# Feed forward: the merge of the heads as three float32r products, with rests taken by VectorE

## The reference, cut to what matters

```python
merged = scaled.transpose(0, 2, 1, 3).reshape(B, S, 2 * E)     # 8192 tokens x 512
return merged @ Wo                                             # 512 x 256
...
x = x + _layernorm(_L0_attn_ref(_layernorm(x), ...))
x = x + _layernorm(_L0_ffn_ref(_layernorm(x), W1, b1, W2, b2)) # 256 -> 1024, gelu, -> 256
```

## Time and profile before

| | us |
|---|---|
| median of 3 runs | 3853.26 (3853.02 to 3857.16) |
| the profiled execution's own time | 3850.38 |
| its span in the profile | 3848.7 |
| PE busy in the span | 3415.3 (89%) |
| DVE busy | 2936.1 (76%) |
| ACT busy | 2231.0 (58%) |

### The profile page before, as it was taken

How to read it: one execution, slowest core, us unless ns; L and a number is a source line. 1 busy time by engine, 2 the same in 40 slices (tenths; PEclk the granted TensorE clock), 3 DMA queues, 4 the chain that set the end, 5 groups by cost and what they waited for, 6 DMA issues and landing times. The chain is left out here.

```text
span 3848.7 us, 67900 instructions
## 1 busy us (share of the span) xinstructions
PE 3415.3 (89%) x22102; PEld 2005.8 (52%) x22102; DVE 2936.1 (76%) x7111; ACT 2231.0 (58%) x4709; POOL 1688.8 (44%) x2993
## 2 busy tenths in 40 slices
PE   5886999999999999999999959999698887969950
PEld 4775444444444444444444428888344444648840
DVE  6765999999999999999999916666377776863348
ACT  4554477777777777777777737776101104635532
POOL 2411266666666666666666641111000003656642
PEclk9998899999999999999999989999899997989975
DMA  5777544444443444534434222220410113335668
GB/s 179 227 226 221 82 84 71 77 80 71 78 77 71 80 74 73 80 72 75 82 71 75 41 72 77 88 88 28 140 44 22 44 33 118 117 129 168 176 188 255
DMA packets 377610, 390.26 MB, mean 101 GB/s; under 512 B 118896, under 2 KB 291824, under 8 KB 375216
## 3 DMA queue, kind: packets, MB, share of 16 engines
q1 hardware_dynamic: 362960, 347.42, 39.0%
q0 software_dynamic: 13728, 37.77, 2.6%
q10 hardware_dynamic: 576, 0.79, 0.1%
HBM read 229.17 MB, written 155.05 MB: 100 GB/s over the span
## 5 line engine op out<-in xcount | busy, mean ns | idle before, releaser
L725 ACT ACTIVATE att_p<-att_st 128x512 f32<-128x512 f32 (+3 forms) x3072 | 1325.3, 492 | 472.1 <-PE att_st L662 452.9
L792 DVE TENSOR_REDUCE att_mcol<-att_ring 128x1 f32<-128x512 f32 (+3 forms) x3072 | 1483.1, 547 | 136.3 <-PE att_ring L640 108.6
L662 PE MATMUL att_st<-att_ops 99*128 99x512 bf16 (+3 forms) x3072 | 915.7, 328 | 4.3 <-ACT att_p L725 3.5
L637 PE MATMUL att_ring<-att_ops 96*128 96x512 bf16 (+3 forms) x3072 | 879.2, 332 | 26.1 <-DMA att_va<-values 23.2
L674 PE MATMUL att_pv<-att_p,att_va 128*32 128x512 f32 (+3 forms) x6144 | 603.3, 495 | 2.0 <-POOL att_p L781 1.3
L781 POOL TENSOR_SCALAR_AFFINE_SELECT att_p<-att_p 128x512 f32<-128x512 f32 x512 | 321.8, 634 | 591.9 <-ACT att_p L725 587.0
L662 PEld LDWEIGHTS att_st<-att_ops 99*128 99x128 bf16 x3072 | 284.9, 98 | 446.0 <-ACT att_p L725 278.8
L640 PE MATMUL att_ring<-c_mask,c_identb 128*128 128x128 bf16 x2048 | 435.2, 222 | 0.0
L637 PEld LDWEIGHTS att_ring<-att_ops 96*128 96x128 bf16 x3072 | 296.8, 98 | 205.1 <-DVE att_mcol L792 79.6
L674 PEld LDWEIGHTS att_pv<-att_p,att_va 128*32 128x32 f32 x6144 | 144.7, 109 | 273.0 <-ACT att_p L725 140.8
L640 PEld LDWEIGHTS att_ring<-c_mask,c_identb 128*128 128x128 bf16 x2048 | 202.9, 99 | 106.2 <-issue 0.6
(11 more groups left out here) (269 smaller groups left out, 6073.8 us busy)
## 6 DMA issues: line engine op xcount, KB each, us to landing
att_ops<-parts SPq DMA_DIRECT2D x1524, 64.0 KB, 3.4
parts<-prj_pt SPq DMA_DIRECT2D x128, 384.0 KB, 4.1
moe_work<-moe_rows SPq DMA_DIRECT2D x79, 260.0 KB, 2.9
values<-prj_vs SPq DMA_DIRECT2D x16, 1024.0 KB, 6.6
att_va<-values SPq DMA_DIRECT2D x64, 256.0 KB, 4.2
heads<-att_ofin SPq DMA_DIRECT2D x128, 128.0 KB, 2.3
ffn_os<-heads SPq DMA_DIRECT2D x16, 1024.0 KB, 4.8
moe_work<-x SPq DMA_DIRECT2D x32, 512.0 KB, 4.3
```

Source lines behind the costliest of these rows:

```text
L637: ins = nc.tensor.matmul(ring[k % NB][:, 0:w], ops[0:KR, s, a, mp, i * P:(i + 1) * P], ops[0:KR, s, a, 2 + mp, c * GN:c * GN + w], start=T ...
L662: nc.tensor.matmul(stp[(t * NST + n) % NS][:, off:GN], ops[:, s, a, 2 + mp, j * P:(j + 1) * P], ops[:, s, a, mp, half * GN + off:(half + 1 ...
L725: act.activation(pr[:, g % R, b, off:GN], stp[(t * NST + n) % NS][:, off:GN], ACT.Exp, scale=SCALE).then_inc(exp_done, 1)
L792: v.tensor_reduce(mcol[:, t % 2, c, col:col + 1], ring[k % NB][:, 0:min(GN, (i + 1) * P - c * GN)], AX.X, ALU.max).then_inc(ring_read, 1)
```

## The change

`wo` is split once into a float32r rounded part `woh` (ACT) and the rest `wol` (DVE). ACT's copy of the turned heads now writes `mt` as float32r, and DVE takes the rest `ml = tp - mt` from the PSUM bank (`merged_low`). The merge is three products, `mt` x `woh`, `ml` x `woh` and `mt` x `wol`, 12 float32r matmuls for a token tile instead of 4 float32 ones. The merge waits for all four rests, and the next user of a bank waits for its rest too. ACT waits for the merges of the group before, before it writes `mt[:, 0]`. On DVE eight `merged_low` stand ahead of `merged_stats(0)`, and in each group with one ahead two stand after `low_part` 0 and two after `low_part` 2.

```diff
--- before.py
+++ after.py
@@ -901,7 +901,8 @@
         m = Mem(nc, ctx, "ffn")
         os_ = m.sb("os", [P, 2, GT, H * VD])
         xs = m.sb("xs", [P, 2, GT, E])
-        mt = m.sb("mt", [P, HC, GN])
+        mt, ml = m.sb("mt", [P, HC, GN]), m.sb("ml", [P, HC, GN])
+        woh, wol = m.sb("woh", [P, HC, E]), m.sb("wol", [P, HC, E])
         x1, xn = m.sb("x1", [P, 3, GT, E]), m.sb("xn", [P, 2, GT, E])
         xt, xl = m.sb("xt", [P, 2, EC, GN]), m.sb("xl", [P, 2, EC, GN])
         hf, ht, hl = m.sb("hf", [P, FM, GN]), m.sb("ht", [P, FM, GN]), m.sb("hl", [P, FM, GN])
@@ -910,9 +911,9 @@
         var, rstd, nmr = m.sb("var", [P, 3, GT]), m.sb("rstd", [P, 3, GT]), m.sb("nmr", [P, 3, GT])
         tp, hp, ya, yo = ([m.ps(f"{n}{i}") for i in range(2)] for n in ("tp", "hp", "ya", "yo"))
         h_loaded, x_loaded, x_stored = m.sems("h_loaded", 2), m.sems("x_loaded", 2), m.sems("x_stored", 2)
-        (own_steps, tp_ready, tp_copied, ya_ready, ya_scale, ya_read, x1_ready, x1_scale, xn_ready,
+        (wo_round, wo_rest, ml_ready, own_steps, tp_ready, tp_copied, ya_ready, ya_scale, ya_read, x1_ready, x1_scale, xn_ready,
          xl_ready, hid_ready, gelu_done, lo_ready, yo_ready, yo_read, y_scale, yf_ready, out_ready) = (m.sem(n) for n in (
-            "own_steps", "tp_ready", "tp_copied", "ya_ready", "ya_scale", "ya_read", "x1_ready", "x1_scale",
+            "wo_round", "wo_rest", "ml_ready", "own_steps", "tp_ready", "tp_copied", "ya_ready", "ya_scale", "ya_read", "x1_ready", "x1_scale",
             "xn_ready", "xl_ready", "hid_ready", "gelu_done", "lo_ready", "yo_ready", "yo_read", "y_scale", "yf_ready", "out_ready"))
         power = Power(C, 0)
         chunks, before, last = turn_order()
@@ -968,7 +969,7 @@
 
         @block.tensor
         def _(pe):
-            pe.wait_ge(C["s_ffn"], 48)
+            pe.wait_ge(wo_rest, 1)
 
             def bank_free(g, c):
                 was = last[g, c]
@@ -977,6 +978,8 @@
                 pe.wait_ge(tp_copied, was + 1)
                 if chunks[was][1] >= HC:
                     pe.wait_ge(xl_ready, chunks[was][0] * EC + chunks[was][1] - HC + 1)
+                else:
+                    pe.wait_ge(ml_ready, chunks[was][0] * HC + chunks[was][1] + 1)
 
             def turn_heads(g, c):
                 if c == 0:
@@ -987,12 +990,13 @@
                 ins.then_inc(tp_ready, 1)
 
             def merge(g, t):
-                pe.wait_ge(tp_copied, turned(g, HC - 1))
+                pe.wait_ge(ml_ready, (g + 1) * HC)
                 if g and t % 2 == 0:
                     pe.wait_ge(ya_read, 4 * (g - 1) + 2 * (t // 2) + 2)
-                for c in range(HC):
-                    ins = nc.tensor.matmul(ya[t // 2][:, t % 2 * E:(t % 2 + 1) * E], mt[:, c, t * P:(t + 1) * P],
-                                           C["wo"][:, c], start=(c == 0), stop=(c == HC - 1))
+                for one, (a, w) in enumerate(((mt, woh), (ml, woh), (mt, wol))):
+                    for c in range(HC):
+                        ins = nc.tensor.matmul(ya[t // 2][:, t % 2 * E:(t % 2 + 1) * E], a[:, c, t * P:(t + 1) * P].bitcast(F32R),
+                                               w[:, c].bitcast(F32R), start=(one == 0 and c == 0), stop=(one == 2 and c == HC - 1))
                 ins.then_inc(ya_ready, 1)
 
             def turn_x(g):
@@ -1049,7 +1053,9 @@
         def _(act):
             def merged(g, c):
                 act.wait_ge(tp_ready, turned(g, c))
-                act.activation(mt[:, c], tp[c % 2][:], ACT.Copy).then_inc(tp_copied, 1)
+                if g and c == 0:
+                    act.wait_ge(ya_ready, g * GT)
+                act.activation(mt[:, c].bitcast(F32R), tp[c % 2][:], ACT.Copy).then_inc(tp_copied, 1)
 
             def x_group(g):
                 for c in range(EC):
@@ -1089,6 +1095,8 @@
                 act.activation(hf[:, n], hp[n % 2][:], ACT.Gelu, bias=C["b1"][:, n:n + 1])
                 act.activation(ht[:, n].bitcast(F32R), hp[n % 2][:], ACT.Gelu, bias=C["b1"][:, n:n + 1]).then_inc(gelu_done, 1)
 
+            act.wait_ge(C["s_ffn"], 48)
+            act.activation(woh[:].bitcast(F32R), C["wo"][:], ACT.Copy).then_inc(wo_round, 1)
             for c in range(HC):
                 merged(0, c)
             for c in range(HC):
@@ -1144,6 +1152,10 @@
                     v.wait_ge(tp_copied, turned(g, HC + c))
                     v.tensor_tensor(xl[:, g % 2, c].bitcast(F32R), tp[c % 2][:], xt[:, g % 2, c], ALU.subtract).then_inc(xl_ready, 1)
 
+            def merged_low(g, c):
+                v.wait_ge(tp_copied, turned(g, c))
+                v.tensor_tensor(ml[:, c].bitcast(F32R), tp[c % 2][:], mt[:, c], ALU.subtract).then_inc(ml_ready, 1)
+
             def low_part(g, n):
                 v.wait_ge(gelu_done, g * FM + n + 1)
                 v.tensor_tensor(hl[:, n].bitcast(F32R), hf[:, n], ht[:, n], ALU.subtract).then_inc(lo_ready, 1)
@@ -1168,6 +1180,12 @@
             for k, work in enumerate(power_order()):
                 nth[work, power_order()[:k].count(work)] = k
 
+            v.wait_ge(wo_round, 1)
+            v.tensor_tensor(wol[:].bitcast(F32R), C["wo"][:], woh[:], ALU.subtract).then_inc(wo_rest, 1)
+            for c in range(HC):
+                merged_low(0, c)
+            for c in range(HC):
+                merged_low(1, c)
             merged_stats(0)
             scales(0, nth["a", 0], ya_scale)
             merged_add(0)
@@ -1186,6 +1204,9 @@
                     scales(2, nth["c", g - 1], y_scale)
                 for n in range(5):
                     low_part(g, n)
+                    if ahead and n in (0, 2):
+                        merged_low(g + 2, n)
+                        merged_low(g + 2, n + 1)
                 if g + 1 < G:
                     x_low(g + 1)
                 low_part(g, 5)
```

## The result

| | before | after |
|---|---|---|
| median on the same chip | 3855.21 us (3853.02 to 3858.43, 4 runs) | 4004.99 us (4003.31 to 4007.33, 4 runs) |
| ratio | | 1.0388, 95% interval 1.037 to 1.0406 |
| profiled execution, its span | 3850.38, 3848.7 | 4003.31, 4001.5 |

The changed kernel is 150 us slower, where 133 were forecast (3986 us, range 3955 to 4030). The spans differ by 152.8 us.

What follows compares the result with a forecast made beforehand. PE's work was taken to bound the stage (24.96 of 25.37 us a group). Start and group 0, 7.8, plus 125 for groups 1 to 13 (+9.6 each, PE's saving included) made 133 us: 3986 us, range 3955 to 4030.

Steps and rivals of the forecast that it cites:

- The first wait: PE's second turns wait for DVE's rest of chunk 0, behind low_part 0: idle 6.7 us, from 8.96 to 15.71.
- The second wait: Merge 0 waits for DVE's rests of chunks 2 and 3, behind low_part 2: about 2 us, start at 22.41.
- The price of the clock: PE at about half clock after the stall at the second turns; period 35.0 us, or 33.9 at full clock.
- My rival for that: Clock falls again in the idle time before merge 0: some +3 us a group, 4025 us; chance 17%.
- Start and group 0: Eight rests ahead of the first merged statistics, then both waits in group 0: +7.8 us by its end.
- the shorter merges of group 1 give back 1.2: At the start, merged statistics come +4.6 us late; group 1's merges recover 1.2, putting low_part(0, 0) at 2318.3.
- PE's work: A merge takes 1.44 us instead of 1.75, 0.3 less; over 64 merges, 19 us of PE's work.
- Covers: Rounding wo and taking its rest hide under the first heads' load: cost 0, or 2.3 us without the cover.
- clock kept: The stall is there but PE's clock stays up behind it: 3971 us; chance 14%.
- DVE's time alone: The stall is absorbed and only DVE's four added rests a group count, +34 us: 3890 us; chance 6%.
- Faster: PE waits for no rest and the whole 19 us come off: 3834 us; needs chunk 0's rest by 8.96; 3%.
- No float32r gain: A product with its weight load takes 0.15 us, merges stay as long as before: 4003 us; chance 4%.

Runs made afterwards that it cites:

- e1: Changed kernel with DVE's rests of chunks 0 and 1 ahead of finish_stats, those of 2 and 3 ahead of low_part 0; 3992.02 us, ratio 1.0211 to before.
- e7: Changed kernel's products, with PE turning chunks 0, 1 behind the previous group's hidden 7, chunks 2, 3 ahead of hidden 0, rests inside DVE's waits; 3848.05 us, ratio 0.9977.
- e4: As e3, plus four DVE subtractions of constants a group at the rests' places, for which nobody waits; 3908.06 us, ratio 0.9986 to before.
- e8: Changed kernel with DVE taking the rests of chunks 2 and 3 ahead of low_part 2 instead of behind it; 3966.64 us, ratio 1.028 to before.
- e9: Order of e7 with the old float32 merge, no rests of the heads, and wo's rounding and rest kept but unused; 3860.97 us, ratio 1.0008 to before.
- e6: Changed kernel with all rests and waits, but the merge as four float32 products of the rounded parts; 4031.21 us, ratio 1.0447 to before.
- e3: Changed kernel's 12 float32r products without DVE's rests of the heads or their waits, mt standing in for ml; 3902.66 us, ratio 0.9975 to before.
- e5: Changed kernel with 26 unused float32r matmuls filling PE's gap ahead of its second turns in a group; 3988.68 us, ratio 1.0334 to before.

## Why the prediction was right, and where its sizes were off

*The first wait*: forecast 6.7 us, second turns at +15.71, at half pace. Measured 6.68 and +15.78 (2575.00 - 2559.22), hidden 2 at +17.37 for 17.03. Right, and e1 and e7 show that it hangs on the place of the rest, not on DVE's load (e4).

*The second wait*: merge 0 at +22.41 behind about 2 us. Measured +22.71, behind 1.58 to 1.64 us in the short groups and 1.75 to 2.14 in the long ones. Right, and e8 shows its cause to be `low_part(g, 2)` ahead of rests 2 and 3.

*The price of the clock*: forecast one fall a group, 35.0 us. The five short groups, 35.2, are that case. In the other eight the clock falls again. My rival for that had the fall itself, but neither how often it comes nor its price: +3 in each group, merge 0 at half pace, where eight groups of 13 are 1.5 longer and merge 0 still starts at full pace. The mean is 36.16, so the periods give 13 x 10.79 = 140 us and not 125; of the 15 missing, 12 are the second fall (8 x 1.5) and 3 the 0.2 of every group. This is the larger of two terms that were off.

*Start and group 0*: forecast +7.8, measured +11.9 (2341.82 for 2329.92; +13.1 counted from the first turn of heads, which came 1.2 earlier). The first statistics start at 2298.66, 0.7 later than forecast. The step that failed is "the shorter merges of group 1 give back 1.2". Before them PE had waited 2.29 us for ACT's `yn`; after, 5.79, and behind it the merges began at half pace. PE at the start, after:

```profile
2303.18 1.20 PE L998 MATMUL ffn_ya<-ffn_woh,ffn_mt 128*128 128x256 f32 x4 [5.79 <-ACT ffn_yn L1066]
2304.17 1.05 PE L998 MATMUL ffn_ya<-ffn_woh,ffn_ml 128*128 128x256 f32 x4
...
2307.58 0.63 PE L998 MATMUL ffn_ya<-ffn_wol,ffn_mt 128*128 128x256 f32 x4
```

The statistics of group 1 start 6.05 late (2311.12 for 2305.07), and `low_part(0, 0)` too (2320.93 for 2314.88), where I had 3.4. The remaining 1.4 come later in group 0: merge 0 starts at 2327.80 behind a wait of 2.36 us, again at half pace, where I had it at full clock.

*PE's work*: the merges' gain was forecast at 0.3 each, 19 us in all. A group shows the forecast size: 1.21 a group (e7 against e9), and the changed kernel, too, is slower without it (e6). Taken alone in the old order (e3) only 0.71 of it shows. My estimate from the Trainium skill (FP8 and Floating Point Precision, TensorE Precision Notes: a true FP32 product is four passes) was 0.44 a merge, some 1.7 a group; the trace doesn't agree, since a float32r product takes 0.12 us with its weight load (12 in 1.41 us in e7, 2471.07 to 2472.48) and not 0.11.

*Covers*: taking the rest of `wo` ended at 2277.96, ahead of the first turn (PE's first turn of heads waits for its DMA, until 2280.49), as forecast. ACT's new wait for the merges cost nothing that a row shows.

*The rivals*: clock kept, 3971, is ruled out by the half pace behind the first wait in every group. DVE's time alone, 3890, is ruled out by e4 (nothing in the periods, 5 us at the start). Faster, 3834, needed DVE at the rest of chunk 0 by +8.96; it was there at +14.95 (2574.17). With the rests in DVE's waits the kernel is faster, by 9 us and not 19: of 13 x 1.21 = 16 us the start takes 6.3 and the order 2. No float32r gain is ruled out by e7 against e9.

## What to carry to other kernels

An operand split in two gives another engine a place in PE's chain: before counting PE's saved microseconds, look up when that engine, by its own order, reaches the new instruction, and compare it with when PE needs the result or the bank. Here 2.4 us of VectorE's work a group were free where they fell into its idle time (e4, but for 5 us at the start), and as a wait they cost 140 us. Put such work into that engine's waits in its chains, and move the producer (the turns) ahead to match. A stall is priced with what follows it: the half clock behind it, and the next wait that it exposes.

## What the runs showed of the hardware that was not expected

The granted clock fell behind much shorter waits than the 6.7 us one: behind 1.75 to 2.14 us in the eight long groups, when PE had been at 1.2 GHz shortly before, and behind 2.36 us in five groups of e5 and 2.29 us at the start of e9, when PE had worked at full clock. It didn't fall behind 1.58 to 1.64 us in the short groups, nor behind the same 2.36 us in the eight other groups of e5 and the same 2.29 us in the kernel before (granted clock 1.00 in 2297.88 to 2302.00, and 0.65 in e9's 2301.65 to 2306.00). So the length of the wait alone doesn't decide it, and what does, the rows don't show. One such fall in a group came with a period 1.4 to 1.5 us longer.
